# Tile 0's divergence on VectorE and adding DMAs, the first source on ScalarE and a DMA, and channel pairs in the convolution's input

## The reference, cut to what matters

```python
g  = relu(_bn(_dwconv(h, wg)))          # h = s; 3x3 depthwise convolutions
g1 = relu(_bn(_dwconv(h, wg1)))
gy, gx = _sobel(h)
Dx = 1.0 / (gy * gy / LAM2 + 1.0);  Dy = 1.0 / (gx * gx / LAM2 + 1.0)
ux = 0.5 * (roll(g, 1, axis=2) - roll(g, -1, axis=2))       # along the width
vy = 0.5 * (roll(g1, 1, axis=3) - roll(g1, -1, axis=3))     # along the channels
E = (ux + vy) * DT                                          # the divergence
D = 1.0 / (1.0 + 2.0 * Bx + 2.0 * By)                       # Bx = Dx * DT, By = Dy * DT
for _ in range(5):
    h = D * (c0 * h0 - 2.0 * E * h + cm_x * roll(h, 1, 2) + cp_x * roll(h, -1, 2)
             + cm_y * roll(h, 1, 3) + cp_y * roll(h, -1, 3)) + D * (2.0 * DT) * s
```

## Time and profile before

| | us |
|---|---|
| median of 3 runs | 305.89 (305.55 to 306.15) |
| the profiled execution | 307.02 |
| its span, from the first to the last instruction | 305.2 |
| VectorE busy | 262.8 |
| TensorE busy | 249.4 |
| ScalarE busy | 121.0 |

### The profile page before, as it was taken

How to read it: one execution, slowest core, us unless ns; L and a number is a source line. 1 busy time by engine, 2 the same in 40 slices (tenths; PEclk the granted TensorE clock), 3 DMA queues, 4 the chain that set the end, 5 groups by cost and what they waited for, 6 DMA issues and landing times.

```text
span 305.2 us, 5297 instructions
## 1 busy us (share of the span) xinstructions
PE 249.4 (82%) x2308; PEld 215.8 (71%) x2308; DVE 262.8 (86%) x221; ACT 121.0 (40%) x197; POOL 10.7 (3%) x29
## 2 busy tenths in 40 slices
PE   0136999999996999823999999999999966698794
PEld 0125799788566559713998999989989956676683
DVE  1899949999959963999999999999999999997721
ACT  2462777749603400500052351523413235335643
POOL 2000000000200000110010010110101000000000
PEclk9999999999999899985999999999999999999799
DMA  7900000000660000093060051619530012000113
GB/s 234 365 15 0 0 3 5 2 0 4 137 137 4 0 0 2 0 206 69 2 137 2 0 105 34 138 17 223 102 76 2 0 52 89 0 0 0 65 74 137
DMA packets 5894, 18.65 MB, mean 61 GB/s; under 512 B 2416, under 2 KB 2672, under 8 KB 4336
## 3 DMA queue, kind: packets, MB, share of 16 engines
q0 software_dynamic: 1296, 9.44, 15.3%
q1 hardware_dynamic: 4288, 8.16, 8.2%
q10 hardware_dynamic: 288, 0.72, 0.8%
HBM read 6.79 MB, written 2.10 MB: 29 GB/s over the span
## 4 chain that ended last, share of the span: by engine, by line
DVE 51%; PE 37%; issue 5%; ACT 2%; DMA 2%; SPq 0%; DVEq 0%; ACTq 0%
DVE ring L820 26%; PE psum L1068 11%; PE psum L1078 9%; PE psum L1015 6%; PE psum L1151 4%; PE psum L1037 4%; DVE coef L580 3%; DVE first_two L905 3%; DVE ring L643 3%; DVE stats L833 3%; DMA ring<-in_x 2%; DVE coef L863 2%; PE psum L986 2%; DVE coef L828 2%; DVE lo_s L658 2%
## 5 line engine op out<-in xcount | busy, mean ns | idle before, releaser
L820 DVE TENSOR_TENSOR ring<-coef,state 128x2048 f32<-128x2048 f32 x51 | 113.5, 2289 | 8.6 <-PE psum L1078 8.3
L1078 PE MATMUL psum<-mats,ring 128*128 128x128 f32 x816 | 96.3, 277 | 19.1 <-DVE ring L820 18.9
L1078 PEld LDWEIGHTS psum<-mats,ring 128*128 128x128 f32 x816 | 90.8, 143 | 23.1 <-DVE ring L820 22.5
L341 ACT ACTIVATE state<-psum 128x1024 f32<-128x1024 f32 x36 | 35.2, 1029 | 99.0 <-PE psum L1078 83.1
L580 DVE SCALAR_TENSOR_TENSOR coef<-coef 128x2048 f32<-128x2048 f32 x16 | 36.6, 2290 | 0.4
L341 ACT ACTIVATE coef<-psum 128x512 f32<-128x512 f32 (+1 forms) x22 | 17.3, 792 | 26.0 <-PE psum L1037 17.4
L1151 PE MATMUL psum<-hi,dense_m 128*128 128x512 f32 x48 | 20.3, 424 | 0.5 <-DVE lo L869 0.5
L1037 PEld LDWEIGHTS psum<-coef,state 32*128 32x128 f32 x672 | 19.1, 187 | 1.3 <-issue 1.3
L1151 PE MATMUL psum<-lo,dense_m 128*128 128x512 f32 x48 | 19.8, 413 | 0.0
L1037 PE MATMUL psum<-coef,state 32*128 32x64 f32 x672 | 19.7, 271 | 0.0
L1068 PE MATMUL psum<-coef,mats 128*128 128x512 f32 (+2 forms) x40 | 17.4, 570 | 2.4 <-ACT first_two L341 2.4
(11 more groups left out here) (122 smaller groups left out, 279.4 us busy)
## 6 DMA issues: line engine op xcount, KB each, us to landing
first_two<-coef POOLq DMA_DIRECT2D x5, 1024.0 KB, 8.1
coef<-coef POOLq DMA_DIRECT2D x4, 1024.0 KB, 7.3
coef<-in_x SPq DMA_DIRECT2D x2, 1024.0 KB, 5.8
coef<-in_wide_taps SPq DMA_DIRECT2D x3, 384.0 KB, 7.6
ring<-in_x SPq DMA_DIRECT2D x2, 512.0 KB, 6.5
ring<-in_x SPq DMA_DIRECT2D x1, 1024.0 KB, 9.7
out<-coef SPq DMA_DIRECT2D x2, 512.0 KB, 3.1
out<-coef SPq DMA_DIRECT2D x4, 256.0 KB, 2.4
```

The lines of the kernel that those rows point to most:

```text
L341: return nc.scalar.activation(dst, src, func, **kw)
L820: V.tensor_tensor(wc(ring[:, slot, :]), wc(coef[:, t, a, :]), h_at(t, k, dw, dc), ALU.mult)\
L1078: ins = mm(slot_ap(name)[:, (j % 8) * 128:(j % 8) * 128 + 128], src[:, j * 128:j * 128 + 128], ident, is_transpose=True, start=first and j ...
```

## The change

1. `scale_grouped` writes neighbouring channels beside each other (g a w e instead of g e a w), the root is written twice per group (64 numbers) so that it can be read in the same order, and `to_depthwise` reads with a step of two.
2. TensorE sums the variance of tile 1 before the last Sobel piece of tile 0; ScalarE makes its root ahead of the last square and of the last 12 scalings of the taps. VectorE's signs of the ternary weights come behind the variance's request. `scale_grouped(1)` comes before tile 0's denominator.
3. Tile 0's divergence: VectorE takes the difference of g1 along the channels into `e0` (the ring's second buffer, `channel_difference`), ScalarE writes minus g, and four accumulating DMAs on POOL's queue add g and minus g, shifted by one column of the image (64 elements), the wrapped column apart. VectorE multiplies `e0` with D (`divergence_added`). TensorE keeps tile 1's divergence alone.
4. Sources: `source` now writes the first source's factor, -(2 + 2 DT) D s. ScalarE copies s into `first_two`, an accumulating DMA adds the source, then ScalarE scales the source down for the later steps. `first_source` on VectorE is gone.
5. `d_of` is split: D, and A0 later. VectorE makes tile 1's diffusivities before tile 0's E. TensorE adds the source of step (0, 0) after the third product, not before the first.

The slots of `early` follow. The diff, cut:

```diff
-             ("gy_0_1", 2), ("gx_0_0", 3), ("gx_0_1", 0), ("var_1", 3), ("cv_0_0", 1), ("cv_0_1", 2), ("cv_0_2", 0),
...
+             ("gy_0_1", 2), ("gx_0_0", 3), ("var_1", 1), ("gx_0_1", 0), ("cv_0_0", 2), ("cv_0_1", 3), ("cv_0_2", 0),
...
+        e0 = ring[:, 1, :]
+        minus_g = state[:, 0, 1, :, :].rearrange("p r q -> p (r q)")[:, 0:N]
...
+            def first_source(t):
+
+                pool.wait_ge(source_ready, t + 1)
+                pool.wait_ge(s_copied[t], 1)
+                pool.dma_start(first_two[t][:, :], coef[:, t, FS, :], accum_op=ALU.add).then_inc(first_full[t], 16)
+
+            pool.wait_ge(e_made, 3)
+            pool.dma_start(e0[:, C:N], gN[0][:, 0:N - C], accum_op=ALU.add).then_inc(e_some, 16)
+            pool.dma_start(e0[:, 0:C], gN[0][:, N - C:N], accum_op=ALU.add).then_inc(e_some, 16)
+            other_rows(0)
+            pool.wait_ge(e_some, 32)
+            pool.wait_ge(minus_ready, 1)
+            pool.dma_start(e0[:, 0:N - C], minus_g[:, C:N], accum_op=ALU.add).then_inc(e_full, 16)
+            pool.dma_start(e0[:, N - C:N], minus_g[:, 0:C], accum_op=ALU.add).then_inc(e_full, 16)
+            other_channels(0)
+            first_source(0)
+            other_rows(1)
+            other_channels(1)
+            first_source(1)
...
+            def copy_s(t):
+
+                copy(wc(first_two[t][:, :]), h_at(t, 0)).then_inc(s_copied[t], 1)
+
+            def source_of(t):
+
+                act.wait_ge(first_full[t], 16)
+                copy(coef[:, t, FS, :], coef[:, t, FS, :], scale=2 * DT / (2.0 + 2 * DT)).then_inc(source_scaled, 1)
...
+            rsqrt_first(128, GROUPS)
             sobel_square(0, 1, 1)
             scale_taps(range(10, 16))
-            rsqrt_first(128, GROUPS)
+            reciprocal_first(0)
             to_natural(0, 0)
             to_natural(0, 1)
-            reciprocal_first(0)
             to_natural(0, 2)
             to_natural(0, 3)
...
+            for q in range(4):
+                wait_reader(act, f"cv_0_{q}")
+            copy(minus_g, gN[0], scale=-1.0).then_inc(minus_ready, 1)
+            sobel_square(1, 0, 0)
+            sobel_square(1, 0, 1)
+            d_of(0)
+            sobel_square(1, 1, 0)
+            sobel_square(1, 1, 1)
             wait_reader(act, "gx_1_0")
             wait_reader(act, "gx_1_1")
             copy(coef[:, 1, 2, :], coef[:, 1, 1, :], bias=(1.0 + 2 * DT) * S).then_inc(shifted_ready, 1)
-            d_of(0)
+            a0_of(0)
...
                 wrap(t, k + 1, halo_ready)
+                if (k, t) == ORDER[0]:
+                    act.wait_ge(ayp_ready, 2)
+                    wait_job(act, "dv_1_1")
+                    copy_s(1)
+                    source_of(0)
+                if (k, t) == ORDER[1]:
+                    source_of(1)
...
             def scale_grouped(t):
 
                 dve.wait_ge(xm_ready, 2 * t + 2)
-                rs = gsum[:, t, 3, :].rearrange("p (a g) -> p a g", a=CP).unsqueeze(3).unsqueeze(4)
-                V.tensor_tensor(s_grouped[t].rearrange("p (g e a w) -> p a g e w", e=2, a=CP, w=W),
-                                h_at(t, 0).rearrange("p w (a g e) -> p a g e w", a=CP, e=2),
-                                rs.broadcast_to([128, CP, CG // 2, 2, W]), ALU.mult).then_inc(s_grouped_ready, 1)
+                rs = root(t).rearrange("p (a g e) -> p a g e", a=CP, e=2).unsqueeze(2)
+                V.tensor_tensor(s_grouped[t].rearrange("p (g a w e) -> p a w g e", e=2, a=CP, w=W),
+                                h_at(t, 0).rearrange("p w (a g e) -> p a w g e", a=CP, e=2),
+                                rs.broadcast_to([128, CP, W, CG // 2, 2]), ALU.mult).then_inc(s_grouped_ready, 1)
...
+            def channel_difference():
+
+                taken_out(0)
+                wait_job(dve, "t2_1_1")
+                e, g1 = wc(e0), wc(g1N[0])
+                V.tensor_tensor(e[:, :, 1:C - 1], g1[:, :, 0:C - 2], g1[:, :, 2:C], ALU.subtract).then_inc(e_made, 1)
+                V.tensor_tensor(e[:, :, 0:1], g1[:, :, C - 1:C], g1[:, :, 1:2], ALU.subtract).then_inc(e_made, 1)
+                V.tensor_tensor(e[:, :, C - 1:C], g1[:, :, C - 2:C - 1], g1[:, :, 0:1], ALU.subtract).then_inc(e_made, 1)
+
+            def divergence_added():
+
+                dve.wait_ge(axp_ready, 1)
+                dve.wait_ge(e_full, 32)
+                V.tensor_tensor(coef[:, 0, AE, :], e0, coef[:, 0, 0, :], ALU.mult).then_inc(ae_ready, 1)
...
-
-            def first_source(t):
-
-                dve.wait_ge(source_ready, t + 1)
-                wait_job(dve, "gx_1_1")
-                stt(wc(first_two[t][:, :]), wc(coef[:, t, FS, :]), (2.0 + 2 * DT) / (2 * DT), h_at(t, 0), ALU.mult,
-                    ALU.add).then_inc(first_two_ready, 1)
+                stt(wc(coef[:, t, FS, :]), wc(coef[:, t, 0, :]), -(2.0 + 2 * DT), h_at(t, 0), ALU.mult, ALU.mult)\
+                    .then_inc(source_ready, 1)
...
+            ternary_sign()
+            rsqrt(128, GROUPS, root(1), wide=True)
+            scale_grouped(1)
             shifted(0)
-            rsqrt(128, GROUPS, gsum[:, 1, 3, :])
             denominator(0)
-            scale_grouped(1)
             scale_s(1)
             split_hi(1)
             split_lo(1)
@@ -918,6 +995,8 @@
             across_columns(0)
             across_rows(0)
             both_diffusivities(0)
+            channel_difference()
+            over_rows(0)
             wait_job(dve, "alpha")
             then(V.reciprocal(wred[:, 5:6], slot_ap("alpha")[:, 1:2]))
             ins = V.tensor_tensor(wred[:, 7:8], slot_ap("alpha")[:, 0:1], wred[:, 5:6], ALU.mult)
@@ -925,17 +1004,16 @@
             dve.wait_ge(alpha_ready, 1)
             leave("alpha")
             denominator(1)
-            over_rows(0)
             over_channels(0)
             newton(1)
-            divergence_taken(0)
             across_rows(1)
-            source(0)
+            across_columns(1)
+            both_diffusivities(1)
+            divergence_added()
             dve.wait_ge(outp_in, 16 * 10)
             ask_rsqrt(V.tensor_scalar(rs_in[:, 0:1], outp[:, 3:4], BN_EPS, None, ALU.add))
-            first_source(0)
-            across_columns(1)
-            both_diffusivities(1)
+            dve.wait_ge(ae_ready, 1)
+            source(0)
...
                 pe.wait_ge(s_grouped_ready, t + 1)
-                turns(f"t2_{t}_{h}", [half(s_grouped[t], h)[:, j * 128:j * 128 + 128] for j in range(CG // 2)])
+                pairs = half(s_grouped[t], h).rearrange("p (g r e) -> p g r e", e=2, r=128)
+                turns(f"t2_{t}_{h}", [pairs[:, j // 2, :, j % 2] for j in range(CG // 2)])
...
 
-            def add_products(t, k, between=()):
+            def add_products(t, k, between=(), first=False):
 
                 count = products_of(k, t)
                 for i in range(count):
                     pe.wait_ge(product, summed[0] + 1)
-                    ins = add_turned(t, k, ring[:, summed[0] % RING, :], False, i == count - 1)
+                    ins = add_turned(t, k, ring[:, summed[0] % RING, :], first and i == 0, i == count - 1)
                     summed[0] += 1
                     if i < count - 1:
                         ins.then_inc(ring_free, 1)
...
-                if last and last[0] < STEPS - 1 and last[1] != t:
-                    add_source(t, k)
+                if last is None:
+                    take_sums(t, k)
+                    add_products(t, k, ((2, lambda: add_source(*reversed(ORDER[0]), False)),), True)
+                    last = (k, t)
+                    continue
+                if last[0] < STEPS - 1 and last[1] == t:
                     back_to_natural(*last)
-                elif last and last[0] < STEPS - 1:
+                take_sums(t, k)
+                add_source(t, k)
+                if last[0] < STEPS - 1 and last[1] != t:
                     back_to_natural(*last)
```

More of the change, by code:

```diff
@@ L465, in _ @@
                     .then_inc(dense_m_ready, 1)
-            for q in range(4):
-                to_natural(1, q)
+            to_natural(1, 2)
+            to_natural(1, 3)
+            wait_job(act, "gx_1_1")
+            copy_s(0)
             rsqrt_first(128, 1)
             d_of(1)
+            a0_of(1)
             def relu_bn_out(t, h):
```

100 lines of the change are left out of this document (53 added, 47 removed), and 5 rows, old and new, of the table early.

## The result

The changed kernel takes 296.9 us in the median of 4 runs (295.85 to 298.04), the kernel before 305.89; the ratio is 0.971, with a 95% interval of 0.967 to 0.975. That is 9.0 us faster where 19.0 were forecast: 10.0 us are missing, and the time lies outside the range. The profiled execution took 296.63 us, its span is 294.8. Two executions of the experiments, of 613.8 us (128x128 matmuls of 536 ns in the mean, against 280 in the changed kernel) and of 356.2 us (at a mean clock of 0.754), are left out of all that follows.

A forecast was written before the change was run, and what follows sets the result against it. VectorE was taken to bound the kernel, with TensorE and ScalarE waits before the second step at 139.61. Terms 3.4 + 3.3 + 3.3 + 7.6 + 4.6 - 2.7 = 19.5, taken as 19.0: 286.9 us, range 285.3 to 290.8.

The forecast's parts named there:

- Channel pairs: VectorE's two scalings into the convolution's layout fall from 4.0 to 2.29 us each: 1.7 us saved, twice.
- Second variance: Earlier variance sum and root for tile 1 remove 3.3 us of VectorE's 3.6 us of waits; 0.3 stays.
- Tile 0's divergence: VectorE gains 2.6 us of work for E and loses a 3.28 us wait; accumulating DMAs hide with 4.5 over.
- Rival 4: Two chained DMA rounds make it slower than before: 313 us at 25 us a round; chance 0.03 with anything like it.
- Sources: Two VectorE operations of 2.29 us move to ScalarE copies and accumulating DMAs, hidden with 3 to 5 us: 4.6 us saved.
- The divergence of tile 1: On TensorE after a 3.8 us idle, starting at mostly 1.2 GHz: 17.1 us, 83.3 to 100.4.
- rival 2: Late helper: E's DMAs at 12.3 us a round, or TensorE's divergence ending late; 2 to 4 us, 289 to 291; chance 0.13.
- The failed step: TensorE's second convolution, tile 1: its two halves take 13.1 us, as tile 0's did, running 66.3 to 79.5.
- The walk: VectorE's operations timed one by one: first product at 95.6 instead of 104.83, second step at 120.7 instead of 139.61.
- between 290 and 305: Whole-kernel times between the named rivals and no change, with no cause named; chance 0.04.

The follow-up runs named there:

- experiment 6: Changed kernel, E's first accumulating DMA pair held until tile 0's row coefficients: with gap filled 287.29 us; with gap left 288.69 once, 295.6 to 298.0 five times.
- experiment 1: Changed kernel with ScalarE's third square of tile 1's Sobel ahead of tile 0's D: 288.61 us, ratio 0.943.
- the best version: The experiment 1 kernel with 16 idle matmuls ahead of tile 1's divergence: 286.7 us, ratio 0.937.
- experiment 5: Changed kernel without E's four accumulating DMAs: gap filled 287.26 us; gap left 288.98, 288.78, 297.78, 296.1, then six at 295.72 to 298.55.
- experiment 4: Changed kernel, gap left, with 18 idle 512-column matmuls between tile 1's two convolution halves: 298.07 us, ratio 0.973.

## Why the prediction was half right

- *Channel pairs, 1.7 us twice:* right. 2.29 us each. Alone they bring 2.1 us by the medians (2.8 by the ratio) at an expectation of 1.9, for the wait in the first step grows to 8.99 from 7.63. The turns read at a step of two take 2.18 instead of 1.97.
- *Second variance, 3.3 us of waits:* right, 0.40 is left, 0.3 was forecast; the new wait of 0.56 for the shift was not. The old order on the new kernel costs 5.0, since the signs of the weights, moved behind the request, no longer stand in the time that TensorE needs: the term is 3.3 of waits only together with that move.
- *Tile 0's divergence, 2.6 us, DMAs hidden with 4.5 over:* right for E itself. The last of their transfers lands near 85.5 (issued 76.75, 8.7 us under way), and without the slow clock VectorE asks at 89.7 (90.36 less its wait of 0.67, experiment 6), so 4.2 were over. Rival 4 never came near. What these DMAs do to TensorE's instructions has no term in the sum.
- *Sources, 4.6 us:* right (4.9).
- *The divergence of tile 1 in 17.1 us with a cold start:* right for the time from its start to its end, 92.74 to 109.91 is 17.2. In experiment 1 it took 18.3 (83.74 to 102.08), and VectorE waited 1.60: rival 2's slow clock, near its price of 1.7. At full clock, in the best version, it took 15.6.
- *The failed step* is the one before it: "the two halves (13.1 us, as from 40.68 to 53.82) run 66.3 to 79.5". They took 23.5. The walk itself had put ScalarE's D ahead of the square, and so TensorE idle in front of them; it counted the gap as delay and gave its clock no price, though it did so one gap later. The runs showed 1.2 GHz in its place. The price is the 5.51 us of VectorE's new wait and the 4.00 in the first step, 9.5 us, against the 9.4 by which the second step starts late. The profiled executions miss 8.6 us (296.63 against 288.0), for the stretch behind that start is 0.9 shorter than before; the medians miss 10.0, because the kernel before was profiled 1.1 us above its median and the changed one 0.3 below. No rival and no end of the range held it: rival 2 looked for the slow clock behind the second gap only, for 1.7 us, and the time fell between 290 and 305, which had a chance of 0.04 and no cause named.
- Behind that gap stood a second, unseen cost of the kind: with the first gap filled, the late instruction block stalls TensorE, and the clock falls in the stall. Either is enough. Filling the gap alone gained nothing (296.94), and taking the late block away alone gained in 3 of 16 executions (the unfilled kernels of experiments 5 and 6). Both together gave the forecast's time, 287.3 against 286.9 (experiment 6). The swap in experiment 1, which moves TensorE 2.3 us further ahead of the late block, gave 288.6, and 286.7 with the idle matmuls ahead of the divergence. That both come so near 286.9 is in part luck: experiment 6 pays 0.67 us at E, and the 286.7 has a divergence of 15.6 us where the forecast kept 17.1.

## What to carry to other kernels

When a change puts an idle gap of TensorE (here about 2 us and more) in front of small matmuls, price what follows at both levels of the clock, up to the next wide matmuls, and let one end of the range stand there. Do the same for shorter stalls within a long run of small matmuls. Look for the operation that TensorE waits for and put it first in its engine's queue; this was worth 8.3 us here (296.9 to 288.61) for two exchanged lines. When a filled gap gains nothing, look for the next gap before dropping the theory, and look at the instruction queue where transfers saturate the DMA engines.

## What the runs showed of the hardware

- A gap of TensorE of 2.21 to 2.24 us lowered the clock in 17 of 20 executions (the changed kernel, and the unfilled ones of experiments 5 and 6), with the same program and the same gap going either way; 3.88 us did it in all four. (The gap is read from four traces, the rest is told by times and mean clocks.) The Trainium skill, in "TensorE: Matmul & The Clock Gate", Part 1, says that the number of a kernel's matmuls that run at the low clock varies from run to run; the two traced executions of experiment 5 agree, 9 us apart.
- It also fell with idle times of 0.32 and 0.51 us ahead of it, at the end of the small matmuls of experiment 1. What sets the moment is not shown.
- Small matmuls kept TensorE busy for 22 us at 1.2 GHz without getting the clock back (the changed kernel); during 18 wide ones it came back (experiment 4).
- 192 matmuls of 32 by 64 take 5.59 us at 2.4 GHz and 10.0 to 10.5 at 1.2.
- A block taken for TensorE's instructions came 4.5 us late behind accumulating DMAs of 1 MB, and TensorE stood still for 3.29 us; with the DMAs issued 4.7 us later it came ahead of them, and the stall was gone.
